# Attention stage of an audio tower: value projections in tiles of 512 columns, TensorE's steps of a slot grouped by kind, and routing steps moved by a slot

## The chip, the cores and the metric

One core of a Trainium2 chip runs the kernel. The metric is the device time of one execution in microseconds (us). Most executions of this kernel lie within 0.3% of each other.

## The reference

32 sequences of 375 frames with 80 features go through a tokenizer (windows of 8 frames, stride 4, two dense layers with relu, a normalisation over the batch), which gives 93 rows of 256 features for each sequence. Then follow one attention block and one mixture-of-experts block:

```python
h = _L0_tok_ref(x, W1, b1, W2, b2, gamma, beta)
h = h + _L0_attn_ref(_layernorm(h), kernel, WO)          # 16 heads of 64, softmax over 93 keys
h = h + _L0_ffn_ref(_layernorm(h), shared_up, shared_down,
                    routed_up, routed_down, router_w)    # 1 shared + 8 routed experts, top 2
```

In attention q, k and v are projections of the normalised rows, scores are scaled and put through a softmax, the probabilities weight the values, and WO maps the 1024 features back to 256. In the second block router logits pick two experts for each row.

## The kernel before, in words

The kernel has three stages: the tokenizer, attention (with the routing of the rows to the experts beside it), and the experts. The change lies in the attention stage.

Attention works on 8 groups (NG) of 4 sequences, 372 rows in each (N = 4 x 93). Most products are made in three passes of a high and a low part (PASSES) of type fp32r; scores, the transposes of the probabilities and the product with the values are plain 4-byte float. A group has 16 heads, taken in 8 pairs j, and NU = 16 slots s, one for each head u. The order of every engine is written out by hand in its own function group(g, behind, ahead), slot by slot; what one engine needs of another is a wait on a semaphore. Beside its own attention, a group does the next group's LayerNorm 1 (ahead) and the last group's LayerNorm 2, router logits and routing (behind).

The steps on TensorE (PE), by their lines:
- qk_tile (L852): one head pair of q or k for the group, 6 matmuls of 372 columns.
- v_tile (L840): values of one sequence b and of VW columns, 6 matmuls. VW is 256 in the kernel before (two head pairs), so a group has 16 such tiles, v00 to v33 (first digit the columns, second the sequence).
- scores (L865), values (L886, o_ps) and output (L898, the product with WO, 9 matmuls of 256 columns), each for a head pair j; turn (L873) transposes the probabilities of a head u.
- rows_tile (L587) transposes the next group's hidden rows, back_tile (L595) turns normalised rows back (z10, z11 for LN1 of the next group, z20, z21 for LN2 of the last), logits_tile (L605, L607) and rank_tile (L616, L618) are the router's.

Projections, row transposes, logits and ranks share the two banks of pj_ps. Bank 0 is emptied by ScalarE (ACT), bank 1 by VectorE (DVE). tiles(kind) lists the order in which the tiles pass through the banks and bank_of says which bank; number() turns that into the value that the semaphores filled and taken must reach. begin() makes TensorE wait until the tile before in the same bank is taken.

A head u goes: scores; DVE's shift (maximum and subtraction, L1105, L1108); ACT's exps (four exponentials with sums, L1002); DVE's total (reciprocal, L1114); GpSimd's (POOL) scaling (L1225); turn; ACT's take_turned (L1009); values for a pair; take_o in two halves, ACT (L1014) and DVE (L1118); output. ACT's normalise_batch (L994) applies the batch normalisation to the next group's rows. DVE's moments, spread and normalise (L658 to L688) and POOL's root (a Newton iteration of 13 small steps) make the LayerNorms. DVE's keep (L707), take_logits (L722), the steps of routing (max, shift, sum, recip, scale, top, index, expert, masks, both, pick, slots) and take_ranks (L757, L773) do the routing. In the last group shared_hi and shared_lo split the first weights of the next stage on ACT and DVE. POOL scatters rows to the experts by indirect DMAs, SP stores the split rows; both are untouched by the change.

In the kernel before, TensorE's even slots hold scores, q and k of the next pair, turn and values; the odd slots hold two value tiles, turn and the output of the pair before. A group's outputs 6 and 7 fall into slots 1 and 3 of the next.

Of the kernel before, what the change touches and what calls it, by code (L numbers as in the profile page):

```python
# [13 lines left out]
P = 128  # L14
# [52 lines left out]
def audio_tower_kernel(nc, x, W1, b1, W2, b2, gamma, beta, qkv_w, WO, sh_up, sh_down, rt_up, rt_down, router_w, out):  # L67
# [6 lines left out]
    TP = SL  # L74
# [24 lines left out]
    with ExitStack() as ctx:  # L99
# [395 lines left out]
        with ExitStack() as c:  # L495
            NU = 2 * NJ
            VW = 2 * P
# [100 lines left out]
            def logits_tile(pe, g, n):  # L598

                pe.wait_ge(taken[0], number(g, "z20"))  # L600
                begin(pe, g, "logits")
                for c in range(C):
                    for m in range(MC):
                        to = pj_ps[0:R, 1, c * 2 * E:(c + 1) * 2 * E]
# [4 lines left out]
                ins.then_inc(filled[1], 1)  # L609
# [19 lines left out]
            def hi(act, g, i, m, n):  # L629

                act.wait_ge(filled[m], number(g, "z%d%d" % (i + 1, m)))
                if i == 0:
                    for b in range(2):
                        if m == 0 and not (isinstance(g, int) and g < 0):
                            act.wait_ge(filled[b], number(g, "v3%d" % (2 + b)))
                elif m == 0 and not (isinstance(n, int) and n == 0):
                    act.wait_ge(stored, n * 16)
                    act.wait_ge(filled[1], number(g, "logits", back=1))
# [137 lines left out]
            def take_logits(dve, g, n):  # L776
                dve.wait_ge(filled[1], number(g, "logits"))
                route(dve, n, "copy", pj_ps[0:R, 1, 0:C * 2 * E].rearrange("p (c s e) -> p c e s", c=C, s=2))
                dve.wait_ge(r_chain, n * R_STEPS + 1)
                dve.sem_inc(taken[1], 1)  # L780
# [51 lines left out]
            def _(pe):  # L832
# [43 lines left out]
                def values(g, j):  # L876
                    if j % 2 == 0:
                        for b in range(2, 4):
                            pe.wait_ge(taken[b % 2], number(g, "v%d%d" % (j // 2, b)))
                    pe.wait_ge(turned_out, g * NU + 2 * (j + 1))  # L880
                    ge(pe, o_lo, g * NJ + j)
                    for b in range(GB):
                        cols = slice(b * TP, (b + 1) * TP)
                        for h in range(2):
                            at = (j % 2) * P + h * DH
                            ins = pe.matmul(o_ps[h * DH:(h + 1) * DH, cols], v_rows[:, (j // 2) % 2, b, at:at + DH],  # L886
# [17 lines left out]
                def group(g, behind, ahead):  # L904
                    V = {0: "00 01", 1: "02 03", 3: "10 11", 5: "12 13", 7: "20 21", 9: "22 23", 11: "30 31", 12: "32 33"}
                    for s in range(NU):
# [7 lines left out]
                        for v in V.get(s, "").split():  # L914
                            v_tile(g, "v" + v)
# [4 lines left out]
                        if s == 1 and ahead:  # L920
                            rows_tile(pe, g, 0, g + 1)
# [6 lines left out]
                        if s == NU - 1 and ahead:  # L928
                            pe.wait_ge(taken[1], number(g, "z11"))
                            qk_tile(g, "q0")  # L930
# [10 lines left out]
                        if s == NU - 1 and behind:  # L941
                            rank_tile(pe, g, g - 1)
                        if s == NU - 1 and ahead:
                            qk_tile(g, "k0")
                        if s == 1 and ahead:
                            rows_tile(pe, g, 1, g + 1)
# [799 lines left out]
```

## Time and profile before

| | us |
|---|---|
| runs (3) | 1139.02 to 1141.57, median 1139.83 |
| the profiled execution | 1139.72 |
| its span | 1138.1 |
| TensorE matmuls busy | 1058.7 (93% of the span) |
| TensorE weight loads busy | 1007.0 (88%) |
| VectorE busy | 585.0 (51%) |
| ScalarE busy | 575.7 (51%) |
| GpSimd busy | 419.3 (37%) |
| mean granted TensorE clock | 0.979 of full |

The span is the time from the first to the last instruction. The busy times of the engines overlap. A matmul's end is modelled in the profile and overlaps the start of the next, so the distance from one start to the next says more of its cost than its length. The groups of the attention stage begin (first scores) at about 110, 168, 234 and then every 66 us; the stage ends at about 643 us.

### The profile page before, as it was taken

To read this page: it belongs to the slowest core of one execution; us is meant where nothing else is said; L and a number is where in the kernel's file an instruction comes from. 1 tells how busy PE (TensorE), PEld (TensorE's weight loads), DVE (VectorE), ACT (ScalarE), POOL (GpSimd) and SP (SyncE) were. 2 spreads that over 40 slices of the span, in tenths; PEclk is the share of its full clock that TensorE was granted. 3 is DMA by queue.
4 is the path that set the end of the run, shared out by engine and by line. 5 is a ranking of instruction groups with operands and counts; after the bars stand their busy time and mean duration, and the time that the engine had idled before them with its cause. 6 is when DMAs were issued, how large, how long until landed. Compare 5 with 4: busy or idle time off the path is not lost. (4 is left out here: it accounts for less than half of the span.)

```text
span 1138.1 us, 27316 instructions
## 1 busy us (share of the span) xinstructions
PE 1058.7 (93%) x9140; PEld 1007.0 (88%) x9141; DVE 585.0 (51%) x1628; ACT 575.7 (51%) x2141; POOL 419.3 (37%) x505
## 2 busy tenths in 40 slices
PE   5994999999999999999999799999999999998998
PEld 5994889889898888989888699999999999998898
DVE  3655556666576566656656655333242332333454
ACT  3542656555554655555555545454454544544252
POOL 2000222234252523425252322423664264153882
PEclk9996999999999999999999799999999999999999
DMA  9517990001000100100011333313331312311653
GB/s 187 131 26 252 354 347 11 29 19 38 9 21 28 27 27 19 36 10 18 28 28 55 97 113 130 120 37 120 120 112 44 120 62 95 120 46 43 160 143 106
DMA packets 81594, 99.24 MB, mean 87 GB/s; under 512 B 29968, under 2 KB 64496, under 8 KB 81520
## 3 DMA queue, kind: packets, MB, share of 16 engines
q1 hardware_dynamic: 57648, 58.87, 17.1%
q0 software_dynamic: 18176, 29.12, 8.8%
q10 hardware_dynamic: 5696, 10.39, 2.6%
q8 instruction: 30, 0.49, 0.2%
q14 instruction: 44, 0.36, 0.1%
HBM read 50.48 MB, written 47.74 MB: 86 GB/s over the span
## 5 line engine op out<-in xcount | busy, mean ns | idle before, releaser
L1225 POOL TENSOR_TENSOR prob<-prob,rc 93x372 f32<-93x372 f32 x128 | 103.0, 805 | 331.1 <-DVE rc L1114 330.8
L852 PE MATMUL pj_ps<-xg,wA 128*128 128x372 f32 x768 | 152.4, 346 | 4.2 <-DVE next_row L773 2.8
L1708 DVE TENSOR_TENSOR act_s<-dn_ps,act_s 128x256 fp32r<-128x256 f32 x112 | 47.6, 425 | 199.8 <-ACT act_s L1587 199.8
L852 PEld LDWEIGHTS pj_ps<-xg,wA 128*128 128x128 f32 x768 | 130.6, 192 | 10.6 <-DVE next_row L773 3.4
L1002 ACT ACTIVATE prob<-prob 93x93 f32<-93x93 f32 x512 | 135.7, 270 | 1.9 <-DVE rc L1114 1.0
L840 PE MATMUL pj_ps<-wB,xg 128*93 128x256 f32 x768 | 106.8, 286 | 0.0
L1009 ACT ACTIVATE probT<-t_ps 93x372 f32<-93x372 f32 x128 | 60.8, 475 | 77.9 <-PE t_ps L873 75.0
L840 PEld LDWEIGHTS pj_ps<-wB,xg 128*93 128x93 f32 x768 | 91.6, 159 | 8.2 <-DVE kT L1086 2.4
L1002 ACT ACTIVATION_READ_ACCUMULATOR prob<-prob 93x1 f32 x512 | 97.8, 191 | 0.0
L982 ACT ACTIVATE qT<-pj_ps 128x372 f32<-128x372 f32 x64 | 30.8, 481 | 128.5 <-PE pj_ps L852 113.3
L898 PE MATMUL y_ps<-wB,oT 128*124 128x256 f32 x576 | 88.4, 297 | 7.5 <-DVE oT L1118 7.5
L1105 DVE TENSOR_REDUCE mx<-s_ps 93x4 f32<-93x372 f32 x128 | 67.2, 525 | 51.2 <-PE s_ps L865 50.8
L1483 PE MATMUL up_ps<-rx,wB 128*128 128x256 f32 x720 | 86.5, 278 | 4.1 <-ACT act_s L1587 2.3
L1483 PEld LDWEIGHTS up_ps<-rx,wB 128*128 128x128 f32 x720 | 84.0, 188 | 5.5 <-ACT act_s L1587 2.9
L1497 PE MATMUL dn_ps<-wB,act_s 128*128 128x256 f32 x720 | 88.6, 282 | 0.0
L1497 PEld LDWEIGHTS dn_ps<-wB,act_s 128*128 128x128 f32 x720 | 85.9, 188 | 0.0
L1587 ACT ACTIVATE act_s<-up_ps 128x256 fp32r<-128x256 f32 x224 | 85.5, 382 | 0.0
L898 PEld LDWEIGHTS y_ps<-wB,oT 128*124 128x124 f32 x576 | 74.8, 190 | 11.5 <-DVE oT L1118 9.7
L1591 ACT ACTIVATE rows_out<-dn_ps 128x512 f32<-128x512 f32 x28 | 16.7, 597 | 129.5 <-PE dn_ps L1497 129.5
L1483 PE MATMUL up_ps<-rx,wA 128*128 128x256 f32 x624 | 75.2, 278 | 4.6 <-ACT act_s L1587 4.6
L1483 PEld LDWEIGHTS up_ps<-rx,wA 128*128 128x128 f32 x624 | 72.8, 188 | 5.9 <-ACT act_s L1587 5.5
L1381 POOL DMA_INDIRECT raw<-slots,slot_q x48 | 63.0, 1312 | 37.5 <-issue 36.5
(175 smaller groups left out, 2106.2 us busy)
## 6 DMA issues: line engine op xcount, KB each, us to landing
slots<-zeros SPq DMA_DIRECT2D x8, 3072.0 KB, 23.6
rows_in<-slots SPq DMA_DIRECT2D x29, 256.0 KB, 2.6
raw<-in_L_ffn_routed_up POOLq DMA_DIRECT2D x7, 1024.0 KB, 5.4
raw<-in_L_ffn_routed_down POOLq DMA_DIRECT2D x7, 1024.0 KB, 8.4
slots<-rows_out ACTq DMA_DIRECT2D x28, 256.0 KB, 2.0
ln_out<-split SPq DMA_DIRECT2D x8, 744.0 KB
frames<-in_x SPq DMA_DIRECT2D x8, 400.0 KB
raw_w<-in_L_attn_kernel SPq DMA_DIRECT2D x6, 512.0 KB, 5.7
```

What stands on the lines that cost most here:

```text
L840: ins = pe.matmul(pj_ps[0:TP, b % 2, 0:VW], xg[:, dp, m, b * TP:(b + 1) * TP], wB[:, wp, at:at + VW], start=(k == 0), stop=(k == 5))
L852: ins = pe.matmul(pj_ps[:, t, 0:N], wA[:, wp, at:at + P], xg[:, dp, m, :], start=(k == 0), stop=(k == 5))
L898: ins = pe.matmul(y_ps[0:R, c // 2, c % 2 * HD:(c % 2 + 1) * HD], oT[:, j % 2, dp, c * R:(c + 1) * R], wB[:, wp, at:at + HD], start=(j == ...
L1002: ins = act.activation(prob[:, u % 4, b, :], prob[:, u % 4, b, :], ACT.Exp, scale=SCALE, accum_out=sm[:, u % 2, b:b + 1])
L1009: act.activation(probT[:, u % 4, :], t_ps[:, 0:4 * TP], ACT.Copy).then_inc(turned_out, 1)
L1105: dve.tensor_reduce(mx[:, u % 2, :], s4, AX, ALU.max).then_inc(max_done, 1)
L1225: pool.tensor_tensor(p, p, rc[:, u % 2, :].unsqueeze(2).broadcast_to([TP, 4, SL]), ALU.mult).then_inc(scaled, 1)
L1381: pool.indirect_dma_start(out=y_ring(b, k), out_offset=None, in_=slots, in_offset=bass.IndirectOffsetOnAxis(ap=slot_q[:, k, b:b + 1], axis ...
L1483: ins = pe.matmul(up_ps[:, f % 4, 0:ET], w[:, wp, at:at + P], rx[:, dp, m, :], start=(k == 0), stop=(k == 5))
L1497: ins = pe.matmul(dn_ps[:, 0, a * HD:(a + 1) * HD], act_s[:, dp, f, a * P:(a + 1) * P], w[:, wp, at:at + HD], start=(k == 0), stop=(k == 3 ...
L1587: act.activation(act_s[:, HI, f, 0:ET], up_ps[:, f % 4, 0:ET], ACT.Gelu).then_inc(rgelu_done, 1)
L1708: dve.tensor_tensor(act_s[:, LO, f, 0:ET], act_ps[f % 2], act_s[:, HI, f, 0:ET], ALU.subtract).then_inc(ract_lo, 1)
```

## The change

- VW becomes 512: four head pairs in a value tile, 8 tiles for a group (v00 to v13) of 6 matmuls with 512 columns each, and v_rows is indexed by the half (j // 4) itself.
- TensorE's order in a slot is new: in even slots scores, q, k, then the output of a pair one half slot later than before (output j in slot 2j + 6; outputs 5, 6 and 7 fall into the next group, output 5 of the last group into drain), logits, the next group's q0, then the value tile, turn, values; in odd slots a value tile, turn and what is left. The value tiles lie in slots 0, 1, 2, 3, 5, 7, 9, 11.
- q0 of the next group goes from slot 15 to 14, rank ahead of the turn of slot 15, rows_tile(1) from slot 1 to 2, logits from the end of slot 11 to slot 10 and from bank 1 to bank 0.
- DVE: add from slot 3 to 4, the moments of LN1 from slot 2 to 3, those of LN2 from slot 4 to 5, normalise of LN2 from 7 to 8, take_logits from 11 to 10, the routing steps one slot earlier (index to both into slot 13), take_ranks ahead of the rest of slot 15. POOL: root of LN2 beside heads 5, 6, 7 instead of 4, 5, 6, that of LN1 in two parts instead of three. ACT: its halves of the same moves; exp of the logits in slot 11.

The core of the diff:

```diff
-            VW = 2 * P
+            VW = 4 * P
...
-                t = ["q1", "k1", "v00", "v01", "v02", "v03"] + ["p10", "p11"] * ahead + ["q2", "k2", "v10", "v11", "q3", "k3"]
-                t += ["v12", "v13", "q4", "k4", "v20", "v21", "q5", "k5", "v22", "v23"]
-                t += ["z20", "z21"] * behind + ["q6", "k6", "v30", "v31"] + ["logits"] * behind + ["q7", "k7", "v32", "v33"]
-                t += ["z10", "z11"] * ahead + ["rank"] * behind + ["q0", "k0"] * ahead
-                return t
+                t = ["q1", "k1", "v00", "v01"] + ["p10"] * ahead + ["q2", "k2", "v02"] + ["p11"] * ahead + ["v03", "q3", "k3"]
+                t += ["v10", "q4", "k4", "v11", "q5", "k5", "v12"] + ["z20", "z21"] * behind + ["q6", "k6"]
+                t += ["logits"] * behind + ["v13", "q7", "k7"] + ["z10", "z11", "q0"] * ahead + ["rank"] * behind
+                return t + ["k0"] * ahead
...
-                return 1 if tile[0] == "k" or tile in ("logits", "rank") else 0
+                return 1 if tile[0] == "k" or tile == "rank" else 0
...
# TensorE, group
-                    V = {0: "00 01", 1: "02 03", 3: "10 11", 5: "12 13", 7: "20 21", 9: "22 23", 11: "30 31", 12: "32 33"}
+                    V = {0: "v00", 1: "v01", 2: "v02", 3: "v03", 5: "v10", 7: "v11", 9: "v12", 11: "v13"}
...
+                        if s % 2 == 0 and s >= 6:
+                            output(g, s // 2 - 3)
+                        elif s % 2 == 0 and behind:
+                            output(g - 1, NJ + s // 2 - 3)
+                        if s == 10 and behind:
+                            logits_tile(pe, g, g - 1)
+                        if s == 14 and ahead:
+                            pe.wait_ge(taken[1], number(g, "z11"))
+                            qk_tile(g, "q0")
+                        if s in V:
+                            v_tile(g, V[s])
+                        if s == NU - 1 and behind:
+                            rank_tile(pe, g, g - 1)
                         if s >= 2:
                             turn(g, s - 2)
                         elif behind:
                             turn(g - 1, NU + s - 2)
-                        if s == 1 and ahead:
-                            rows_tile(pe, g, 0, g + 1)
+                        if s == NU - 1 and ahead:
+                            qk_tile(g, "k0")
+                        if s in (1, 2) and ahead:
+                            rows_tile(pe, g, s - 1, g + 1)
...
-                        if s in (13, 14):
-                            output(g, 4, range(0, 2) if s == 13 else range(2, C))
-                        elif s % 2 and s >= 5:
-                            output(g, (s - 5) // 2)
-                        elif s in (1, 3) and behind:
-                            output(g - 1, NJ - 2 + s // 2)
...
# DVE, routing and group
-                    plan = {12: ("max", "shift", ""), 13: ("sum", "recip", "scale top"), 14: ("", "", "index expert"),
-                            15: ("", "masks both", "pick slots")}
+                    plan = {11: ("max", "shift", ""), 12: ("sum", "recip", "scale top"), 13: ("index", "expert", "masks both"),
+                            15: ("", "", "pick slots")}
...
-                            if s == 7:
+                            if s == 8:
                                 normalise(dve, g, 1, g - 1, x_rows)
```

## Rows read from the trace of the kernel before

**Rows 1.** The windows view: window, length, PE, PEld, DVE, ACT, POOL busy, PEclk, DMA share, GB/s

```profile
300.00:366.00 66.00, 63.47 (x620) 58.04 (x619) 42.41 (x132) 37.05 (x177) 25.56 (x48) 1.00 0.08 24
...
614.00:643.00 29.00, 20.36 (x185) 17.71 (x186) 17.68 (x53) 13.69 (x50) 4.01 (x5) 0.80 0.08 27
```

**Rows 2.** The timeline of PE, a pair of slots: start, length, engine, line, op

```profile
320.05 0.49 PE L873 MATMUL t_ps<-ident,prob 93*93 93x93 f32 x4
320.47 0.87 PE L886 MATMUL o_ps<-probT,v_rows 93*64 93x93 f32 x16
321.26 1.64 PE L840 MATMUL pj_ps<-wB,xg 128*93 128x256 f32 x12
322.75 0.49 PE L873 MATMUL t_ps<-ident,prob 93*93 93x93 f32 x4
...
324.36 0.82 PE L865 MATMUL s_ps<-kT,qT 64*93 64x93 f32 x14
```

**Rows 3.** The timeline of PE at the end of a group

```profile
165.08 1.22 PE L898 MATMUL y_ps<-wB,oT 128*124 128x256 f32 x9
166.14 1.19 PE L852 MATMUL pj_ps<-xg,wA 128*128 128x372 f32 x6
```

**Rows 4.** The chain that ended last: start, length, what

```profile
666.49 8.17 PE up_ps L1443 x48
...
736.61 5.44 PE up_ps L1483 x48
```

**Rows 5.** The timeline of PE, slots 1 and 12 to 15 of two groups

```profile
306.48 0.49 PE L873 MATMUL t_ps<-ident,prob 93*93 93x93 f32 x4
307.78 0.65 PE L587 MATMUL pj_ps<-ident,hs 128*124 128x128 f32 x4 [0.81 <-ACT v_rows L988]
...
352.98 0.49 PE L873 MATMUL t_ps<-ident,prob 93*93 93x93 f32 x4
...
363.97 2.31 PE L852 MATMUL pj_ps<-xg,wA 128*128 128x372 f32 x12 [0.47 <-DVE next_row L773]
```

**Rows 6.** The timeline of PE, slot 13 of the first group

```profile
158.07 0.80 PE L595 MATMUL pj_ps<-ident,z_rows 124*128 124x124 f32 x6
...
159.50 0.74 PE L898 MATMUL y_ps<-wB,oT 128*124 128x256 f32 x4 [0.63 <-DVE oT L1118]
```

**Rows 7.** The timeline of DVE, slots 12 to 15

```profile
355.43 0.55 DVE L1118 TENSOR_TENSOR oT<-o_ps,oT 128x372 fp32r<-128x372 f32 x1 [1.78 <-ACT oT L1014]
...
356.27 1.00 DVE L696 TENSOR_TENSOR xg<-pj_ps,xg 128x372 fp32r<-128x372 f32 x2
...
357.89 0.54 DVE L1105 TENSOR_REDUCE mx<-s_ps 93x4 f32<-93x372 f32 x1
...
358.93 0.16 DVE L1114 RECIPROCAL rc<-sm 93x4 f32<-93x4 f32 x1
...
361.06 0.16 DVE L741 COPY p_q<-tops 124x6 f32 x1
...
362.18 0.67 DVE L753 TENSOR_TENSOR both<-mask 124x24 fp32r<-124x24 f32 x1
...
363.54 0.18 DVE L757 TENSOR_TENSOR rank<-pj_ps,next_row 124x24 f32<-124x24 f32 x1 [0.69 <-PE pj_ps L618]
```

**Rows 8.** The timeline of ACT and DVE: longer steps

```profile
306.18 1.28 ACT L994 ACTIVATE hs<-h_s,bn_shift,bn_scale 128x372 f32 x2
...
308.56 0.60 ACT L627 ACTIVATE h_s<-pj_ps 124x512 f32 x1 [0.47 <-PE pj_ps L587]
...
332.85 1.06 DVE L688 TENSOR_SCALAR x_rows<-h_s,row_mv,row_r 124x256 f32 x3 [2.11 <-POOL row_r L64]
```

**Rows 9.** The timeline of PE in the last group and the drain

```profile
618.42 0.49 PE L873 MATMUL t_ps<-ident,prob 93*93 93x93 f32 x4
...
639.09 2.28 PE L898 MATMUL y_ps<-wB,oT 128*124 128x256 f32 x9 [1.16 <-DVE oT L1118]
```

**Rows 10.** The windows view of the drain

```profile
632.00:634.00 2.00, 0.39 (x3) 0.42 (x4) 2.00 (x4) 0.85 (x1) 0.80 (x1) 0.50 0.00 0
```

More of the change, by code:

```diff
@@ L634, in hi @@
                         if m == 0 and not (isinstance(g, int) and g < 0):
-                            act.wait_ge(filled[b], number(g, "v3%d" % (2 + b)))
+                            act.wait_ge(filled[b], number(g, "v1%d" % (2 + b)))
                 elif m == 0 and not (isinstance(n, int) and n == 0):
                     act.wait_ge(stored, n * 16)
-                    act.wait_ge(filled[1], number(g, "logits", back=1))
+                    act.wait_ge(filled[0], number(g, "logits", back=1))
                 to = (xg, split2)[i]
@@ L776, in take_logits @@
             def take_logits(dve, g, n):
-                dve.wait_ge(filled[1], number(g, "logits"))
-                route(dve, n, "copy", pj_ps[0:R, 1, 0:C * 2 * E].rearrange("p (c s e) -> p c e s", c=C, s=2))
+                dve.wait_ge(filled[0], number(g, "logits"))
+                route(dve, n, "copy", pj_ps[0:R, 0, 0:C * 2 * E].rearrange("p (c s e) -> p c e s", c=C, s=2))
                 dve.wait_ge(r_chain, n * R_STEPS + 1)
-                dve.sem_inc(taken[1], 1)
+                dve.sem_inc(taken[0], 1)
             def scatter(pool, n, i, x):
@@ L884, in values @@
                         for h in range(2):
[L885 to L886 removed]
+                            at = (j % 4) * P + h * DH
+                            ins = pe.matmul(o_ps[h * DH:(h + 1) * DH, cols], v_rows[:, j // 4, b, at:at + DH],
                                             probT[:, (2 * j + h) % 4, cols], start=True, stop=True)
@@ L934, in group @@
                             values(g - 1, NJ + s // 2 - 2)
-                        if s in (13, 14):
-                            output(g, 4, range(0, 2) if s == 13 else range(2, C))
-                        elif s % 2 and s >= 5:
-                            output(g, (s - 5) // 2)
-                        elif s in (1, 3) and behind:
-                            output(g - 1, NJ - 2 + s // 2)
[L941 to L946, printed above, removed]
-                        if s == 11 and behind:
-                            logits_tile(pe, g, g - 1)
                 def start():
@@ L963, in drain @@
                     g = NG - 1
+                    output(g, NJ - 3)
                     turn(g, NU - 2)
@@ L986, in take_v @@
                     take(g, tile)
-                    ge(act, pv_done, g * NJ + 2 * (jj - 1))
-                    act.activation(v_rows[:, jj % 2, b, :], pj_ps[0:TP, 0, 0:VW], ACT.Copy).then_inc(taken[0], 1)
+                    ge(act, pv_done, g * NJ + 4 * (jj - 1))
+                    act.activation(v_rows[:, jj, b, :], pj_ps[0:TP, 0, 0:VW], ACT.Copy).then_inc(taken[0], 1)
                 def normalise_batch(n):
@@ L1020, in group @@
                             take_q(g, s // 2 + 1, g)
-                        if s == NU - 1 and ahead:
+                        if s == 14 and ahead:
                             take_q(g, 0, g + 1)
@@ L1028, in group @@
                             take_turned(g - 1, NU + s - 2)
-                        if s == 1 and ahead:
-                            take_rows(act, g, 0, g + 1)
+                        if s in (1, 2) and ahead:
+                            take_rows(act, g, s - 1, g + 1)
                         if s == 9 and behind:
@@ L1131, in group @@
                             shift(g, s)
+                        if s == NU - 1 and behind:
+                            take_ranks(dve, g, g - 1)
                         if behind:
@@ L1152, in group @@
                             take_o(g - 1, NJ + s // 2 - 2)
-                        if s == NU - 1 and behind:
-                            take_ranks(dve, g, g - 1)
                         if s == NU - 1 and ahead:
                             take_k(g, 0, g + 1)
-                        if s == 3 and behind:
+                        if s == 4 and behind:
                             add(g - 1)
                         if ahead:
-                            if s == 2:
+                            if s == 3:
                                 moments(dve, g, 0, g + 1)
-                            if s == 3:
                                 spread(dve, 0, g + 1)
@@ L1226, in group @@
                                            ).then_inc(scaled, 1)
-                        if u in (4, 5, 6) and behind:
-                            root(pool, 1, g - 1, THIRDS[u - 4])
-                        if u in (7, 8, 9) and ahead:
-                            root(pool, 0, g + 1, THIRDS[u - 7])
+                        if u in (5, 6, 7) and behind:
+                            root(pool, 1, g - 1, THIRDS[u - 5])
+                        if u in (8, 9) and ahead:
+                            root(pool, 0, g + 1, (range(1, 8), range(8, ROOT_STEPS))[u - 8])
                         if scattering:
@@ L1515, in _ @@
                 down(wA, 2, range(0, 2))
-                pe.wait_ge(taken[0], number(LG, "z20"))
+                pe.wait_ge(taken[0], number(LG, "logits"))
                 turn_rows(0)
```

31 lines of the change are left out of this document (12 added, 19 removed).

## The prediction, made before the changed kernel was run

> **What bounds the kernel now.** I read the stretches first, then TensorE in order of time, then what the other engines do while it waits. The change touches the attention stage alone, about 109 to 643 us of the span. [...]
>
> In the ordinary pairs of slots one run of matmuls follows the other without a gap [rows 2]. The gaps of a group lie in two places: before the transposes of the next group's rows (start to start 1.30 us where four head transposes take 0.35, so 0.95 idle), and in the stretch from turn(10) in slot 12 to the k0 tile in slot 15, 352.98 to 363.97, 10.99 us [rows 5].
>
> **TensorE's own work.** Two terms.
>
> First, the order. A run of matmuls costs more after some lines than after others. output (L898) comes now after turn's transposes: turn and output together take 324.36 - 322.75 = 1.61 us, the way into the scores included [rows 2]. Where output follows a projection it takes 166.14 - 165.08 = 1.06 us [rows 3]. After the change seven of a group's outputs follow a k tile, and the scores follow a turn. The way from a turn into narrow 4-byte matmuls is in the rows too: 320.47 - 320.05 = 0.42 us [rows 2]. 1.61 against 1.06 + 0.42 = 1.48 gives 0.12 to 0.13 us, seven times: **-0.84 us** a group. The other changes of kind are as many as before: a value tile after values in six odd slots, scores into projection, turn into values. Ends of the cost: 0, if the penalty moves to another run, and -1.0.
>
> Second, the value tiles. 12 matmuls of 256 columns become 6 of 512. The 12 take 322.75 - 321.26 = 1.49 us [rows 2], of which about 0.08 is the slow first one after values, so 0.118 each. No matmul of 512 columns is in the trace. [...] 12 x 0.118 - 6 x 0.230 = 0.03 us for a wide tile, eight a group: **-0.24 us**; ends +0.1 and -0.75. [...]
>
> The copies of the values get wider and fewer: ACT's copy of 512 columns takes 0.60 us [rows 8]. Neither engine is near full [rows 1], so that costs nothing but latency, which counts below.
>
> **The waits of a middle group.** I followed the new order with the distances of slot 12: turn(10) starts at 352.98 [rows 5], and DVE's half of take_o at 355.43 [rows 7], 2.45 us later, because ACT does take_turned, four exps and its own take_o first. DVE is free again at +2.92 (355.90).
>
> - Slot 9, back tiles of LN2. normalise moves from slot 7 to slot 8, where it stands behind take_o(2). So it starts 2.92 us after turn(6) and takes 1.06 [rows 8]: TensorE can start at +4.05. Until then TensorE has turn 0.42, values 0.79 [rows 2], a wide value tile 1.46 and a turn 0.33, 3.0 us. **+1.05 us**, new. This is the largest single term of the loss. In exchange DVE's wait for POOL's root goes, which was hidden.
> - Slots 1 and 2, rows_tile. In slot 0 ACT has the wide v00 (some 0.50 until the next starts), take_turned, exps, take_o and two LN1 affines of 1.28 us in all [rows 8]: affine at +3.88 after turn(14), TensorE there at +3.0: 0.88. rows_tile(1) in slot 2 now follows v02 and a turn, and shares the bank with v02: copy done 0.25 + 0.60 us after the tile, TensorE there at 0.33, so 0.55. Together 1.43 against 0.95 now: **+0.46**.
> - Slots 10 and 12: logits sit in ACT's bank and are released by DVE behind take_o(3) and keep; q7 waits about 0.17, q6 about 0.1 for the lo half. Small waits of today of the same kind (0.15) go. **+0.12**.
> - Slots 12 to 15. Here the moved routing steps count. After turn(10) DVE has take_o to +2.92, scale and top 0.70 (what lies from the lo pair to 357.89), index, cast, a reciprocal and the masks 1.1 (361.06 to 362.18), the two lo halves 1.0, both 0.67, then shift(14) 1.04 (357.89 to 358.93) [rows 7]: shift(14) is done at +7.5. ACT's exps(14) and take_o(5) need 1.5 more, DVE's take_o(5) 0.47, and take_ranks releases k0 0.43 after its start (363.54 to 363.97) [rows 5, 7]: **k0 starts at +10.0**. TensorE has 7.5 us of work there (three turns 0.42, 0.42, 0.40 and a last 0.33, two values 0.79, back tiles 0.61, scores 0.95, an output behind them 1.17, q0 1.03, rank 0.55), so 2.5 us of gaps (q0 behind the lo half, turn(13), above all k0 behind the ranks). Now the stretch is 10.99 us and holds one output more, 1.1 us: 9.9. So the gaps before output(4), which go, are bought back by the DVE queue: **+0.1**.
>
> Sum of a middle group: -0.84 - 0.24 + 1.05 + 0.46 + 0.12 + 0.1 = **+0.65 us**; six such groups, **+3.9 us**. scatter, the loads and stores and SP's queue stay in place; POOL's root runs a slot later, behind scale(7), whose reciprocal DVE gives before take_o(2), so it is in time for the normalise in slot 8.
>
> **First group.** It has no ranks, no LN2 and no logits. Four outputs after k tiles, -0.48; the wait before output(4) goes (the back tiles to it 159.50 - 158.07 = 1.43 us for 0.61 of work [rows 6]) and one of about 0.65 before turn(13), -1.5 in all, with nothing behind them; rows_tile waits longer (only two wide value tiles cover the affines), paid for by the narrower start, about 0. **-2.0 us**.
>
> **Last group.** Up to slot 12: +1.05 + 0.27 for the same waits, -1.0 of own work, no rows tiles: **+0.3**. From turn(10) to the end of output(7) the kernel of before takes 641.3 - 618.4 = 22.9 us, in which TensorE waits for DVE (both, behind shared_lo) and for the last scales, and the clock falls to 0.50 [rows 9, 10]. The same walk, from turn(10): output(4) at +3.1, turn(12) +5.4 (index now ahead of its reciprocal), rank +6.6, turn(13) +7.6, output(5) as filler +8.6, turn(14) +11.25 behind take_ranks and shared_lo(0), turn(15) +13.3, output(6) +13.8, values(7) +14.9, output(7) +17.0, end +18.1 at full clock. TensorE still idles over 1 us three times, so I let the clock fall as now; output(6), values(7) and output(7) at half of it (an output 2.28 for 1.1 us [rows 9]) add 2.7: 20.8. **-2.1 us**, ends 0 and -6.
>
> **Sum**: +3.9 - 2.0 + 0.3 - 2.1 = +0.1 us. The profiled execution took 1139.72 us, the median of the runs is 1139.83: **1139.8 us**. A measurement of this kernel can tell about 0.2% (2.3 us) from no change. Own range of this case 1137 to 1143.
>
> **Rivals.**
>
> *Faster by the wide tile and the tail, 1133.5.* [...] Chance 0.32.
>
> *Slower by DVE's queue in slots 10 to 15, 1146.* Each 0.1 us on that chain is 0.1 us of TensorE in six groups, since k0 and q0 hang on it. The z_rows normalise, keep, logits, v13 and two routing steps now fall in the shortest slot (11, 1.9 us), and DVE ops next to POOL's can be longer. 1.0 us more a group gives +6 us: 1145.8. It decides from 0.4 us a group. For it: the order puts index, expert, top and scale ahead of lo. Against: I used DVE's measured steps, some of them already beside POOL's. Chance 0.28.
>
> *That it does nothing* (the slow first matmul after a turn moves to another run, so the order gains 0): +5 us, part of the second rival.
>
> **How the numbers follow.** Forecast 0.40, faster rival 0.32, slower rival 0.28. The range must reach into both, 1133.5 to 1146; the likeliest case alone has 1137 to 1143. Faster by over 0.2%: the first rival and a little of the forecast, 0.35; slower: the second and a little, 0.29; within: 0.36.
>
> **What would show it.** Right: output runs of 1.06 us after k tiles; a gap of about 1 us before the LN2 back tiles in slot 9, waiting for x_rows; k0 waiting 1 us for next_row; a group of about 66.6 us against 66.0 now; no wait before output(4) in the middle groups; wide matmuls 0.23 us apart. Wrong: if the group falls under 65.5 us, the waits are shorter than the walk says; if over 67.3 us, DVE's chain was longer; if the wide ones stand 0.22 apart, the first rival's price holds.

## The result, and the profile after

| | before | after |
|---|---|---|
| median of the runs timed side by side (4 each) | 1140.09 us | 1146.88 us (1145.48 to 1150.49) |
| ratio, 95% interval | | 1.0059 [1.0036, 1.0083] |
| profiled execution | 1139.72 | 1150.49 |
| its span | 1138.1 | 1148.8 |
| mean granted TensorE clock | 0.979 | 0.970 |

The kernel became slower by 0.6%. The forecast was 1139.8 us, and 1146.88 lies 0.9 us beyond the upper end of its range. The profiled execution is the longest of the four, 3.6 us above their median, so its span shows 10.7 us of difference where the medians show 6.8. Its mean granted clock is 0.970; the two shortest runs, 1145.48 and 1145.62 us, have 0.973.

The page after, its first line, and from the costliest groups the q/k tiles and the value tiles (busy us, mean ns of one, then idle us ahead and what ended most of it):

```profile
span 1148.8 us, 26394 instructions
...
L851 PE MATMUL pj_ps<-xg,wA 128*128 128x372 f32 x768 | 161.5, 361 | 14.7 <-DVE next_row L772 7.4
...
L839 PE MATMUL pj_ps<-wB,xg 128*93 128x512 f32 x384 | 102.5, 403 | 0.0
```

The value tiles are the half as many matmuls that the diff promises, and they wait for nothing. The q and k tiles carry the largest part of the loss: 14.7 us idle ahead of them, and each modelled 361 ns long, though their shape is unchanged. Before, the page had 4.2 us and 346 ns for them.

Where the 10.7 us lie, by the distances between the first scores of one group and of the next:

| stretch | before | after | difference |
|---|---|---|---|
| up to the first scores | | | +0.65 |
| first group | 58.67 | 55.22 | -3.45 |
| second group | 65.99 | 67.54 | +1.55 |
| five groups more | 65.93 to 65.97 | 68.27 to 68.31 | +11.6 |
| last group, to the last matmul of output(7) | 76.87 | 74.54 | -2.3 |
| the experts | | | +2.7 |

So a middle group costs 2.3 us more where the forecast had 0.65. The first of these differences holds a shift of work: output(5) now falls into the next group (1.07 us), so like for like the first group gained 2.4 us and the last one 3.4.

The longest waits of TensorE over the third to seventh group (engine, tile and line, releaser: us in total, times, longest):

```profile
PE pj_ps L851 <- DVE next_row L772: 6.2, 5, 1.2
PE pj_ps L594 <- DVE x_rows L687: 4.6, 5, 0.9
PE pj_ps L851 <- DVE xg L695: 4.4, 5, 0.9
PE pj_ps L586 <- ACT hs L990: 3.9, 5, 0.8
PE pj_ps L586 <- ACT v_rows L984: 1.8, 5, 0.4
```

TensorE in order of time in one such group after the change, to be read beside [rows 2, 5] (start, duration, engine, line, operation, count, idle before and releaser):

```profile
308.54 0.49 PE L872 MATMUL t_ps<-ident,prob 93*93 93x93 f32 x4
309.81 0.65 PE L586 MATMUL pj_ps<-ident,hs 128*124 128x128 f32 x4 [0.78 <-ACT hs L990]
...
313.40 1.22 PE L897 MATMUL y_ps<-wB,oT 128*124 128x256 f32 x9
314.45 1.55 PE L839 MATMUL pj_ps<-wB,xg 128*93 128x512 f32 x6
315.84 0.49 PE L872 MATMUL t_ps<-ident,prob 93*93 93x93 f32 x4
316.69 0.43 PE L586 MATMUL pj_ps<-ident,hs 128*124 128x128 f32 x2 [0.35 <-ACT v_rows L984]
...
340.75 0.49 PE L872 MATMUL t_ps<-ident,prob 93*93 93x93 f32 x4
342.17 0.85 PE L594 MATMUL pj_ps<-ident,x_rows 124*128 124x124 f32 x6 [0.93 <-DVE x_rows L687]
...
355.86 0.49 PE L872 MATMUL t_ps<-ident,prob 93*93 93x93 f32 x4
...
361.41 1.28 PE L851 MATMUL pj_ps<-xg,wA 128*128 128x372 f32 x6 [0.88 <-DVE xg L695]
...
364.19 0.55 PE L872 MATMUL t_ps<-ident,prob 93*93 93x93 f32 x4
365.98 3.67 PE L851 MATMUL pj_ps<-xg,wA 128*128 128x372 f32 x12 [1.24 <-DVE next_row L772]
369.58 1.04 PE L864 MATMUL s_ps<-kT,qT 64*93 64x93 f32 x16
```

Three things can be read from these lines. An output behind a k tile takes 314.45 - 313.40 = 1.05 us, as in [rows 3]. The waits stand where the forecast put them: 342.17 - 340.75 = 1.42 us for a turn of 0.33, so 1.09 before the back tiles, and k0 starts 365.98 - 355.86 = 10.12 us after turn(10). And one thing was not forecast: the 12 matmuls of k0 and q1 take 369.58 - 365.98 = 3.60 us, where before they took 366.21 - 363.97 = 2.24 (the run of 12 in [rows 5] starts at 363.97, and the scores behind it start at 366.21).

The windows around them (busy us of PE, PEld, DVE, ACT, POOL, then the granted clock, DMA share, GB/s):

```profile
364.00:366.00 2.00, 0.76 (x9) 0.60 (x8) 0.87 (x4) 2.00 (x13) 0.00 (x0) 1.00 0.00 0
366.00:368.00 2.00, 2.00 (x8) 2.00 (x9) 0.09 (x2) 0.48 (x4) 0.80 (x1) 0.62 0.00 0
368.00:370.00 2.00, 2.00 (x12) 1.58 (x12) 1.10 (x6) 0.23 (x1) 0.00 (x0) 0.52 0.00 0
370.00:372.00 2.00, 2.00 (x25) 1.91 (x22) 1.20 (x3) 0.25 (x1) 0.00 (x0) 1.00 0.00 0
```

The granted clock is 1.00 up to 366, 0.62 and 0.52 in the next two windows (read in steps of half a microsecond: 0.50 from 366.5 to 369.5), and 1.00 again from 370. A middle group of the kernel before stays at 1.00 [rows 1]. The lower clock costs 3.60 - 2.24 = 1.36 us in k0 and q1, and some 0.15 in the scores behind them (0.98 us to the next start for 0.83).

The clock falls in all six middle groups (0.58 in 230 to 234, 0.57 in 298 to 302 and 366 to 370, 0.60 in 434 to 438, 0.63 in 502 to 506, 0.66 in 570 to 574), the second group included:

```profile
229.44 3.67 PE L851 MATMUL pj_ps<-xg,wA 128*128 128x372 f32 x12 [1.16 <-DVE next_row L772]
233.03 0.63 PE L864 MATMUL s_ps<-kT,qT 64*93 64x93 f32 x6
```

Its k0 and q1 take 3.59 us as well. That group is shorter than the next five because its waits are: 0.57 us of idle ahead of q0 for 0.88, 1.16 ahead of k0 for 1.24, 0.85 ahead of the back tiles for 0.93, and less before the rows tiles.

What releases k0, on DVE:

```profile
365.10 0.55 DVE L1112 TENSOR_TENSOR oT<-o_ps,oT 128x372 fp32r<-128x372 f32 x1 [1.30 <-ACT oT L1010]
365.56 0.17 DVE L756 TENSOR_TENSOR rank<-pj_ps,next_row 124x24 f32<-124x24 f32 x1
365.76 0.16 DVE L772 TENSOR_TENSOR next_row<-next_row,pj_ps 124x8 f32<-124x8 f32 x1
```

The ranks lie in bank 1 from 364.19 on. DVE stands still for 1.30 us, waits for ACT's half of take_o(5), does its own half, and only then takes the ranks and frees the bank.

The last group gained more than forecast, and the reason was in the kernel before. Its timeline, TensorE, in that group's slot 3:

```profile
579.47 0.54 PE L873 MATMUL t_ps<-ident,prob 93*93 93x93 f32 x4 [1.70 <-POOL prob L1225]
579.79 1.82 PE L898 MATMUL y_ps<-wB,oT 128*124 128x256 f32 x9
581.54 1.57 PE L865 MATMUL s_ps<-kT,qT 64*93 64x93 f32 x16
```

A turn waited 1.70 us for POOL's scaling, and behind it an output took 1.75 us for 1.26 and the scores 1.49 for 0.83: the same loss of clock, with 0.50 granted from 580.5 to 583.5. After the change no wait for prob in this group is over 0.9 us, and its clock from 574.4 to 627 is 1.00. From the first scores to turn(10) it takes 53.00 us instead of 54.34, though it holds output(5) more. From turn(10) to the end of output(7) it takes 649.38 - 627.43 = 21.95 us, before 641.37 - 618.42 = 22.95.

### The profile page after: what moved, and what is told of

It reads as the page before. It is cut to its first block and busy times, and to the rows that moved or that the text cites. A ratio compares the mean times of both kernels' runs of the same rounds, so it can differ in the third digit from the quotient of the medians.

```text
span 1148.8 us, 26394 instructions
## 1 busy us (share of the span) xinstructions
PE 1060.2 (92%) x8756; PEld 984.1 (86%) x8757; DVE 574.0 (50%) x1596; ACT 571.8 (50%) x2109; POOL 420.3 (37%) x505
## 5 line engine op out<-in xcount | busy, mean ns | idle before, releaser
L851 PE MATMUL pj_ps<-xg,wA 128*128 128x372 f32 x768 | 161.5, 361 | 14.7 <-DVE next_row L772 7.4
L851 PEld LDWEIGHTS pj_ps<-xg,wA 128*128 128x128 f32 x768 | 137.2, 201 | 24.6 <-DVE next_row L772 8.3
L839 PE MATMUL pj_ps<-wB,xg 128*93 128x512 f32 x384 | 102.5, 403 | 0.0
L1112 DVE TENSOR_TENSOR oT<-o_ps,oT 128x372 fp32r<-128x372 f32 x64 | 34.9, 546 | 121.1 <-ACT oT L1010 121.0
L897 PE MATMUL y_ps<-wB,oT 128*124 128x256 f32 x576 | 82.4, 289 | 2.5 <-DVE oT L1112 2.5
L897 PEld LDWEIGHTS y_ps<-wB,oT 128*124 128x124 f32 x576 | 77.6, 191 | 4.0 <-DVE oT L1112 3.3
L839 PEld LDWEIGHTS pj_ps<-wB,xg 128*93 128x93 f32 x384 | 56.7, 159 | 23.9
```

What stands on the lines that cost most here:

```text
L839: ins = pe.matmul(pj_ps[0:TP, b % 2, 0:VW], xg[:, dp, m, b * TP:(b + 1) * TP], wB[:, wp, at:at + VW], start=(k == 0), stop=(k == 5))
L851: ins = pe.matmul(pj_ps[:, t, 0:N], wA[:, wp, at:at + P], xg[:, dp, m, :], start=(k == 0), stop=(k == 5))
L897: ins = pe.matmul(y_ps[0:R, c // 2, c % 2 * HD:(c % 2 + 1) * HD], oT[:, j % 2, dp, c * R:(c + 1) * R], wB[:, wp, at:at + HD], start=(j == ...
```

## The experiments

Ten kernels ran. The first four ran beside 23 runs of the kernel before (median 1140.26), the next four beside 14 (1139.9), the last two beside 13 (1140.56). None leaves out a part of the computation. Each has the trace of one execution.

**k0 ahead of the ranks.** After, with slot 15 in the order turn, k0, rank on TensorE, DVE and in the list of tiles:

```diff
-                t += ["logits"] * behind + ["v13", "q7", "k7"] + ["z10", "z11", "q0"] * ahead + ["rank"] * behind
-                return t + ["k0"] * ahead
+                t += ["logits"] * behind + ["v13", "q7", "k7"] + ["z10", "z11", "q0", "k0"] * ahead + ["rank"] * behind
+                return t
...
-                        if s == NU - 1 and behind:
-                            rank_tile(pe, g, g - 1)
...
+                        if s == NU - 1 and behind:
+                            rank_tile(pe, g, g - 1)
```

> The changed kernel with the k0 tile ahead of the rank tile in slot 15 (TensorE: turn, k0, rank; DVE: take_k, then take_ranks). Theory: the 1.45 us gap before k0 goes in six groups, and with it the fall of the granted clock behind it, which doubles the distance of the next matmuls (k0, q1 and the scores 3.6 us instead of 2.24). That is 1.4 + 1.3 us a group, 16 us in six: about 1130 to 1132 us, groups of 65.5 us. Rival (the clock falls because of all the gaps of slots 13 to 15 together, the one before q0 too): only the gap itself goes, 8 us, about 1138, clock still under 1 at the group's end. Rival (DVE's queue is the bound, the wait only moves to k1 or the scores): no change, 1146.

Measured: 1138.2 us (8 runs), ratio 0.998 [0.9962, 0.9999]; groups of 66.5 us. TensorE in slot 15:

```profile
361.71 1.26 PE L851 MATMUL pj_ps<-xg,wA 128*128 128x372 f32 x6
363.77 0.28 PE L615 MATMUL pj_ps<-both,before_w 124*124 124x32 f32 x1 [0.80 <-DVE kT L1080]
```

The gap didn't go, it moved behind k0 and is 363.77 - 361.71 = 2.06 less the 1.10 of k0's own run, 0.96 us long instead of 1.44, so the 1130 to 1132 us of the theory weren't reached. Yet a group became 1.8 us shorter: 0.5 is gap, and the rest clock, which now stays at 1.00 in all middle groups (114 to 626 us). This one swap brings the whole change back to about the time of before.

**LN2's normalise ahead of take_o in slot 8.** After, with two lines moved on DVE:

```diff
+                        if s == 8 and behind:
+                            normalise(dve, g, 1, g - 1, x_rows)
...
-                            if s == 8:
-                                normalise(dve, g, 1, g - 1, x_rows)
```

> The changed kernel with the LN2 normalise of slot 8 ahead of DVE's half of take_o(2). Theory: the back tiles of slot 9 no longer wait 1.09 us for x_rows in seven groups; POOL's root ends about 1.7 us after turn(6), so TensorE finds them ready: -7 us, about 1140. Rival (POOL's root is the late one, as DVE's wait of 2.1 us for it in slot 7 of the kernel before shows): half of it stays, about 1143. Rival (the gap moves behind take_o(2) to q6 or logits): no change.

Measured: 1143.13 us (10 runs), ratio 1.0025 [1.0008, 1.0043]. The wait before the back tiles fell from 1.09 to 0.52 us, no further, since another one stood behind it, for ACT's copy of v12:

```profile
339.50 0.86 PE L594 MATMUL pj_ps<-ident,x_rows 124*128 124x124 f32 x6 [0.35 <-ACT v_rows L984]
```

The time is that of the first rival, the reason isn't POOL's root but this copy. Five of the groups took 67.26 to 67.76 us, the second 0.3 and the others 0.6 to 1.0 less than after. One took 66.64: in it the clock did not fall (1.00 from 362 to 368), though k0 waited 1.45 us as in the others. So the fall doesn't hang on the wait before k0 alone.

**Wide tiles in the old order.** Before, with VW = 512, v_rows indexed by j // 4, and the tiles in slots 0, 1, 2, 3, 5, 7, 9, 11:

```diff
-            VW = 2 * P
+            VW = 4 * P
-                    V = {0: "00 01", 1: "02 03", 3: "10 11", 5: "12 13", 7: "20 21", 9: "22 23", 11: "30 31", 12: "32 33"}
+                    V = {0: "00", 1: "01", 2: "02", 3: "03", 5: "10", 7: "11", 9: "12", 11: "13"}
```

> The kernel before with nothing but the wide value tiles (eight tiles of 512 columns, in slots 0, 1, 2, 3, 5, 7, 9, 11). Theory: a wide tile costs 6 x 0.232 us against 12 x 0.118, so 0.02 us saved 64 times, 1 to 2 us; the empty slot 12 gives its cover away. 1138 to 1142. Rival (the wide tile is what makes the changed kernel slow, by its longer copies in the shared banks): 1144 or more.

Measured: 1142.56 us (10 runs), ratio 1.0033 [1.0015, 1.005]; groups of 66.4 to 66.5 us, clock 1.00. The wide matmuls stand 0.231 us apart, so TensorE's own work shrinks by the forecast's 0.03 us a tile. But with one tile in a slot instead of two, the engines that work meanwhile have less cover: the turn of slot 13 waits 0.6 us, and logits and ranks wait longer. Wide tiles alone cost 0.5 us a group. The trace is that of the shortest of the ten executions (1139.95 us); what made others as long as 1147.64 it can't show.

**Narrow tiles in the new order.** After, with VW = 256 and the tiles in pairs ("00 01" to "32 33", the last in slot 11), v_rows with four buffers.

> The changed kernel with value tiles of 256 columns again, two in each place of a wide one. Theory: the order makes the loss, not the width: 1146 to 1149, the gaps before the LN2 back tiles, q0 and k0 as they are. Rival (the width makes it): back to 1140.

Measured: 1175.8 us (4 runs), ratio 1.0303 [1.0277, 1.033]. The expectation missed. TensorE in slot 11, and DVE at that time:

```profile
358.60 2.87 PE L839 MATMUL pj_ps<-wB,xg 128*93 128x256 f32 x12 [2.80 <-DVEq L779]
```

```profile
356.96 0.55 DVE L1112 TENSOR_TENSOR oT<-o_ps,oT 128x372 fp32r<-128x372 f32 x1 [2.95 <-ACT oT L1010]
357.42 0.95 DVE L706 TENSOR_TENSOR h_s<-h_s,x_rows 124x768 f32 x1
358.29 0.20 DVE L721 TENSOR_REDUCE ex<-pj_ps 124x24 f32<-124x48 f32 x1
```

Tile v32 goes to bank 0, where the logits of slot 10 lie until DVE has done take_o, keep and take_logits. The real change has one tile there, v13, in bank 1. So this kernel has a conflict that neither before nor after has, and is no measure of the order alone. Narrow tiles in the new order with other banks were not run.

**The ranks in bank 0.** After, with rank in ACT's bank, which has slack at that point; DVE frees it:

```diff
-                return 1 if tile[0] == "k" or tile == "rank" else 0
+                return 1 if tile[0] == "k" else 0
-                to = pj_ps[0:R, 1, 0:(C + 1) * E]
+                to = pj_ps[0:R, 0, 0:(C + 1) * E]
```

(and the same bank in take_ranks, its semaphores, and the last stage's wait)

> The changed kernel with the rank tile in ACT's bank 0 (as the logits are), so that k0 follows the turn without waiting for next_row; q1 of the next group waits for the ranks instead, with k0 as cover. Theory: of the 1.4 us gap 0.3 is left (before q1), and the granted clock stays at its upper level at the group's end: -1.1 and -1.35 us in six groups, about 1132, groups near 65.8 us; better than k0 ahead of rank (66.5), where 0.96 us came back before rank. Rival (the clock falls because of the number of gaps, not of that one's size): groups of 67.2, about 1140.

Measured: 1134.05 us (4 runs), ratio 0.9952 [0.9935, 0.9968]; groups of 65.77 us, clock 1.00. TensorE in slot 15:

```profile
360.18 0.55 PE L872 MATMUL t_ps<-ident,prob 93*93 93x93 f32 x4
360.51 1.26 PE L851 MATMUL pj_ps<-xg,wA 128*128 128x372 f32 x6
361.97 1.29 PE L851 MATMUL pj_ps<-xg,wA 128*128 128x372 f32 x6 [0.20 <-DVE next_row L772]
```

k0 follows the turn at once, and q1, which now waits for the ranks, does so for 1.46 - 1.10 = 0.36 us. A group is 2.5 us shorter than after: 1.1 of wait, the rest the clock's. The wait before k0 is the link between the change and the loss.

**All covers together.** The kernel above, with the normalise ahead of take_o in slot 8, ACT's LN1 affines (normalise_batch) at the head of slot 0 behind take_q, and rows_tile(1) behind the values of slot 2 instead of ahead:

```diff
-                        if s in (1, 2) and ahead:
-                            rows_tile(pe, g, s - 1, g + 1)
+                        if s == 1 and ahead:
+                            rows_tile(pe, g, 0, g + 1)
...
+                        if s == 2 and ahead:
+                            rows_tile(pe, g, 1, g + 1)
...
+                        if s == 0 and ahead:
+                            normalise_batch(g + 1)
```

> The changed kernel with rank in bank 0, the LN2 normalise ahead of take_o(2), ACT's affines in slot 0 right behind take_q, and rows_tile(1) behind the values of slot 2. Theory: the gaps before k0 (1.1 of 1.4), the LN2 back tiles (0.5 of 1.09), rows_tile (0.95 and 0.52) go together, as each stands alone on TensorE's path: groups of 63.6 to 64.2 us against 65.97 of the kernel before, 1118 to 1126. Rival (DVE's queue in slots 12 to 15 sets the group, and what is saved elsewhere is waited for there): groups no shorter than 65.5, 1131 or more.

Measured: **1119.13 us** (1118.63 to 1121.7, 4 runs), ratio 0.9827 [0.9807, 0.9846]. It beats both kernels. One of its groups, and what TensorE still waits for in five:

```profile
227.00:290.50 63.50, 61.81 (x570) 53.79 (x570) 41.05 (x126) 36.52 (x173) 25.77 (x48) 1.00 0.09 26
```

```profile
PE pj_ps L851 <- DVE xg L695: 4.4, 5, 0.9
PE pj_ps L594 <- ACT v_rows L986: 1.8, 5, 0.4
PE pj_ps L851 <- DVE next_row L772: 0.9, 5, 0.2
```

The waits of a group are down to q0's 0.9 us of idle and small ones, and a group takes 63.6 us, 2.4 below the kernel before. Not all of that is the change's: the kernel before waits some 0.95 us a group before its own rows tiles [rows 5], and no run gave it these covers. A comparison of the two orders, each with its waits covered, was not made.

**DVE late for the ranks, in the kernel before.** Two idle DVE operations (onto a scratch tile) ahead of its wait for the ranks:

```diff
+                            for to in idle:
+                                z = zero_c[:, 0:1].broadcast_to([P, N])
+                                dve.tensor_tensor(to[:, :], z, z, ALU.add)
```

> The kernel before with two idle DVE operations of 372 columns ahead of take_ranks in slot 15, so that the gap before k0 grows from 0.61 to about 1.5 us. It prices the clock by itself. If a k0 gap as in the changed kernel is what lets the granted clock fall, a group grows by 0.9 + 1.35 us (seven groups, six with k0: about +13 us, 1153); if the fall also needs the 1.0 us gap before q0 shortly ahead, by 0.9 only (+5.5 us, 1146).

Measured: 1139.61 us (10 runs), ratio 0.9994 [0.9984, 1.0004]; groups 0.13 us longer. The operations fell into 0.69 us in which DVE had nothing to do, so k0's wait only grew from 0.62 to 0.75 us, and the run doesn't answer the question it was made for. It has another answer, though. In its last group the turn of slot 3 waits for POOL as in the kernel before, and here the clock does not fall: the output behind it takes 1.24 us, and from 575 to 623 us the granted clock is 1.00.

```profile
581.94 0.54 PE L874 MATMUL t_ps<-ident,prob 93*93 93x93 f32 x4 [1.56 <-POOL prob L1229]
582.26 1.30 PE L899 MATMUL y_ps<-wB,oT 128*124 128x256 f32 x9
583.50 0.90 PE L866 MATMUL s_ps<-kT,qT 64*93 64x93 f32 x16
```

**The rows tiles alone.** After, with only the part of the combined kernel that covers rows_tile.

> The changed kernel with the rows_tile part alone mended: ACT's affines in slot 0 right behind take_q, rows_tile(1) behind the values of slot 2. Theory: the gaps of 0.95 and 0.52 us go in six groups (and 1.8 us in the first): -10 us, about 1137, the rest of a group unchanged. Rival (the earlier affines delay v00, the turn and the exps of slot 0, and the time comes back in slots 1 to 3): less than half of that, 1142 or more.

Measured: 1132.26 us (5 runs), ratio 0.9936 [0.9903, 0.997]. Both waits went, 1.47 us a group, but the kernel gained 14.6 us, not the 9 to 10 of the forecast. The rest is clock: in its trace it falls behind k0's wait in two of the six middle groups (0.50 from 225.0 to 228.0 and from 358.5 to 361.0), not in all, though that wait is unchanged (1.15 to 1.24 us of idle). Groups without it take 65.2 us, the three that it touches 65.9 to 66.2 (the second fall lies across the end of one group and the start of the next). So the wait before k0 and the runs around it, which are the same in all of them, don't decide on the fall by themselves.

**The wait before k0, in the kernel before.** The two idle operations again, now between the arrival of the ranks and their use, so that they delay the release of bank 1 and nothing else of the change is there:

```diff
                 route(dve, n, "rank", pj_ps[0:R, 1, 0:(C + 1) * E])
+                if not (isinstance(g, int) and g >= NG - 1):
+                    for to in idle:
+                        z = zero_c[:, 0:1].broadcast_to([P, N])
+                        dve.tensor_tensor(to[:, :], z, z, ALU.add)
```

> The kernel before with two idle DVE operations of 372 columns between the arrival of the ranks and their use, so that TensorE's gap before k0 grows from 0.61 to about 1.5 us (in the run with the same operations ahead of that wait they fell into DVE's own idle time). Theory (a gap of that size lets the granted clock fall by itself): groups of 65.97 + 0.93 + 1.35 = 68.2 us, about 1153 us. Rival (the gap alone costs; the fall in the changed kernel needs the 1.04 us gap before q0 shortly ahead, where this order has 0.8 and 0.6 spread out): groups of 66.9, 1145.5.

Measured: 1151.62 us (4 runs), ratio 1.0091 [1.0068, 1.0114]; five groups of 68.4 us. TensorE at k0, and a window behind it:

```profile
370.02 3.85 PE L857 MATMUL pj_ps<-xg,wA 128*128 128x372 f32 x12 [1.38 <-DVE next_row L778]
```

```profile
370.00:372.00 2.00, 1.98 (x7) 1.98 (x8) 0.00 (x0) 0.00 (x0) 0.00 (x0) 0.57 0.01 4
```

k0 and q1 take 3.78 us for 2.24, the clock is at 0.57, and a group is 2.4 us longer: 0.9 of wait and 1.5 of clock. The fall comes with the wait before k0 in the old order and with narrow tiles too. It is no property of the new order. But it comes in five of six groups: in the second one k0 waits as long, the clock is 1.00 from 234 to 240, k0 and q1 take their 2.24 us, and the group only grows by the wait, to 66.98 us.

```profile
234.78 2.31 PE L857 MATMUL pj_ps<-xg,wA 128*128 128x372 f32 x12 [1.39 <-DVE next_row L778]
```

**The same delay behind k0.** The kernel with the ranks in bank 0, with the same two operations, so that q1 waits instead of k0.

> The kernel with rank in bank 0 (1134.05) with the same two idle DVE operations between the arrival of the ranks and their use, so that a gap of 0.44 us before q1 grows to about 1.37, 1.1 us of matmuls (k0) later than the one of the changed kernel. Theory (the fall needs two gaps of over 1 us within 5 us): the clock falls again at the group's end: groups of 65.75 + 0.93 + 1.35 = 68.0, 1148. Rival (the k0 matmuls between them keep the clock up, as with k0 ahead of rank): groups of 66.7, 1139.6.

Measured: 1139.67 us (10 runs), ratio 0.9993 [0.9976, 1.001]; groups of 66.07 to 66.69 us, the last 67.46:

```profile
360.02 1.27 PE L856 MATMUL pj_ps<-xg,wA 128*128 128x372 f32 x6
362.39 1.30 PE L856 MATMUL pj_ps<-xg,wA 128*128 128x372 f32 x6 [1.10 <-DVE next_row L777]
363.62 0.90 PE L869 MATMUL s_ps<-kT,qT 64*93 64x93 f32 x16
```

q1 waits 2.37 - 1.10 = 1.27 us, and runs at a granted clock of 1.00 afterwards (360 to 366; 363.62 - 362.39 = 1.23 us for 6 matmuls and the switch); only the last of the six middle groups lost clock (0.50 from 563.0 to 566.0). The delay added 0.9 us to a group and no more. Two waits of over a microsecond close to each other, q0's 1.04 and this one, are thus not enough. The wait came out some 0.2 us shorter than the 1.44 before k0 in the changed kernel, so the run leaves two readings: k0's 1.1 us of work ahead of the wait keeps the clock up, or the wait is just short enough. It shows neither.

## Why the prediction was wrong, point by point

**The failed step.** A middle group of the kernel before has a granted clock of 1.00 [rows 1], and the prediction keeps it there: the sum of a middle group, "-0.84 - 0.24 + 1.05 + 0.46 + 0.12 + 0.1 = +0.65 us", has no term for the granted clock, although the same walk gives k0 a large part of "2.5 us of gaps" and the tail is priced with a fall. In the profiled execution all six middle groups lose 1.36 us that way in k0 and q1, and some 0.15 behind them, 8 to 9 us of its 10.7. Taking the wait from before k0 gives the clock back (ranks in bank 0, 1134.05, 1.00 from 114 to 622 us), and putting it into the kernel before takes the clock there in five groups of six (1151.62). This is shown. How many of the six falls the median run has (1146.88 us, 6.8 above before) no trace shows; the two shortest runs have a mean clock of 0.973 for 0.970, and 0.003 of 1145 us is 3.4 us, by this estimate about two falls of 1.5 us less. The prediction's own [rows 10] and the 1.70 us wait of the last group before would have given the price.

**Own work, the order.** Right. An output behind a k tile takes 1.05 to 1.07 us, forecast 1.06. Added up by distances, with the waits and the clock taken off, a middle group has about 62.3 us of TensorE's work before and 61.2 after: 1.1 us less, an estimate, where the two terms of the forecast make 1.08.

**Own work, the wide tile.** Right. No run shows the 0.230 us that the sum counts for a wide matmul, an estimate of the author's; in its place the trace after shows a median distance of 0.232 us (0.224 to 0.235). From 372 columns (0.170 us, [rows 4]) to 512 that is 0.44 ns a column, where the step from 256 (0.113 us) to 372 takes 0.49. The 0.22 that was to be the first rival's sign did not come.

**The waits.** The terms are right within 0.15 us: back tiles 1.09 (forecast 1.05); rows tiles 0.95 and 0.52 (0.88 and 0.55; their sum less today's 0.95 is 0.48, not 0.46); k0 at +10.12 after turn(10) (+10.0). The 2.5 us of gaps there came as 1.04 before q0 and 1.44 before k0, where the sign named had been 1 us before k0. q7 and q6 wait 0.16 and 0.15, and one turn 0.17, some 0.2 more than the net 0.12. The group came to +2.3: +0.65, the clock's 1.5, and the rest over these small terms. The sign "over 67.3 us, DVE's chain was longer" came up with groups of 68.3, but its reading was wrong: the chain has the length walked, the clock behind it was missing.

**First group.** Forecast -2.0, measured -2.4 like for like. That output(5) leaves it for the next group, and comes back at the last one, was not told apart, which changes no sum.

**Last group.** Forecast +0.3 up to turn(10). Measured -1.34 with output(5) more in it, so -2.4 like for like. The step failed for the other side of the same omission: the idle of 1.70 us for POOL and the clock behind it, about 3 us, went, and the forecast had not looked at it. That the clock falls there is itself not certain: in the two kernels with a late DVE that have the old order, it stays at 1.00 behind a wait of 1.73 and of 1.83 us for 1.86. The tail gained 1.0 us, not 2.1. Its clock falls already ahead of output(5), not at output(6): it is 1.00 up to 636, 0.57 in the next microsecond and 0.50 from 637 to 651.

```profile
636.24 2.28 PE L897 MATMUL y_ps<-wB,oT 128*124 128x256 f32 x9 [0.60 <-DVE oT L1112]
```

**The experts, +2.7.** The change doesn't touch this stage. A gather there took 6.04 us to land for 4.83, and a run of 57 matmuls behind it, a part of it at the lower clock (0.50 from 1067 to 1069, where the same run before had 1.00 throughout), 8.56 us for 7.22. The profiled execution is also 3.6 us above the median of its runs; I take this part for chance, but no run was made to settle it.

**The rivals.** The slower rival's number, 1145.8, is near the result by luck, its mechanism is not what happened: DVE's chain from turn(10) to k0 is 0.1 us longer than walked, not 1.0 us a group. Its place was right, though, since the wait before k0 is where that chain ends. The faster rival is out by the wide tile, 0.232 us a matmul, and by the tail, where the clock falls as before: 0.50 from 637 to 651 us, in the kernel before from 632 to 648. That the order gains nothing is out by the outputs.

**Open.** What exactly makes the clock fall. The table holds what was seen in one trace of each kernel. A wait is here the distance to the next start less the run's own time, which is 0.14 to 0.21 us more than the idle time in the views:

| kernel | wait | work and waits just before | clock behind it |
|---|---|---|---|
| before, last group, slot 3 | 1.86 | over 13 us of unbroken work | falls to 0.50 |
| DVE late for the ranks, the same place | 1.73 | the same | stays at 1.00 |
| before with a late release, the same place | 1.83 | the same | stays at 1.00 |
| after, k0 | 1.38 to 1.45 | a wait of 0.74 to 1.04 at q0, then 3.1 us of short runs | falls to 0.50 in all 6 middle groups |
| normalise ahead of take_o, k0 | 1.36 to 1.45 | as after | falls to 0.50 in 5 of 6 |
| rows tiles covered, k0 | 1.37 to 1.45 | as after | falls to 0.50 in 2 of 6 |
| before with a late release, k0 | 1.5 | three waits of 0.3 to 0.8 in slots 13 to 15 | falls to 0.50 in 5 of 6 |
| k0 ahead of the ranks | 0.96 | k0's 1.1 us | stays at 1.00 in all |
| ranks in bank 0, late release, q1 | 1.27 | k0's 1.1 us | stays at 1.00 in 5 of 6, falls to 0.50 in one |

No kernel varied the wait in small steps. In the same program one group falls and the next does not, and a wait of 1.83 us left the clock at 1.00 where one of 1.27 was followed by 0.50, so the length of the wait alone doesn't decide it. With one trace of each kernel the counts are single draws.

## What to carry to other kernels

When a wait of 1.4 us or so is moved or made, price the clock behind it as well as the wait: here 1.4 us of wait could cost 1.4 us more in the dozen matmuls that followed. Take it as a chance and not as a fixed cost, since the same wait left the clock at 1.00 in other groups (one of six with the normalise ahead of take_o, four of six with the rows tiles covered). A small tile that one engine fills and a busy one empties belongs in the bank whose next user comes later: ranks in bank 0 turned a loss of 0.6% into a gain of 0.5%. And a reordering whose parts are right one by one is worth finishing wait by wait, since with most of its waits covered and the ranks' bank moved the same change gave 1.7%, though some of these covers might have served the kernel before as well.

## What the runs showed of the hardware that was not expected

- The granted clock fell from 1.00 to 0.50 behind some of TensorE's waits of 1.27 to 1.86 us (the table above) and was back at 1.00 some 4 us after the wait's end: in the kernel after k0 starts at 365.98 and the clock is 0.50 from 366.5 to 369.5, in the kernel before the turn starts at 579.47 and it is 0.50 from 580.5 to 583.5.
- Whether it falls behind a wait of 1.4 us differs from group to group of one execution with the same instructions (a group takes 66.6 us at 1.00 against 67.3 to 67.8 with a fall to 0.50 where the normalise is ahead of take_o, 67.0 against 68.4 in the kernel before with a late release, 65.2 against 66.0 with the rows tiles covered). The runs of these kernels spread over 0.4 to 0.8%, while the four of the kernel with the ranks in bank 0 spread over 0.03%. That the falls are a reason for it is a guess that no trace shows; they can't be the only one, since the kernel before, with no fall at k0 in its trace, spreads over 0.5%.
- The step that joins the two routing masks (both) takes DVE 0.18 us after the change and 0.67 before. What differs is POOL: before, one of its scalings runs at the same time (362.00 to 362.81, both from 362.18 to 362.85), after the change none does. Wide tiles in the old order have both cases in one trace, 0.67 us beside a scaling and 0.18 in a group where POOL stands still:

```profile
230.91 0.81 POOL L1225 TENSOR_TENSOR prob<-prob,rc 93x372 f32<-93x372 f32 x1 [2.08 <-DVE rc L1114]
231.09 0.67 DVE L753 TENSOR_TENSOR both<-mask 124x24 fp32r<-124x24 f32 x1
...
298.10 0.18 DVE L753 TENSOR_TENSOR both<-mask 124x24 fp32r<-124x24 f32 x1
```

The long one ends with the scaling, at 231.76 for 231.72 us, and so it does in the kernel before, at 362.85 for 362.81. No run was made on the cause.
